# Attention sums of a graph network: one-hot tiles split between ScalarE and VectorE, all loads issued by SyncE into rings of eight

## The reference

```
a  = exp(a - amax[edge_dst])                                   # one weight per edge and head
ns = segment_sum(vs * a / segment_sum(a)[dst], edge_dst)       # 64 scalar features
nv = segment_sum(vv * a / segment_sum(a)[dst], edge_dst)       # 32 vectors of 3 components
```

## Time and profile before

| what | value |
|---|---|
| median of 3 runs | 12143.02 us (12134.39 to 12146.55) |
| profiled execution, its own time | 12142.17 us |
| profiled execution, its span | 12140.4 us |
| busy over the whole span: PE, DVE, ACT, POOL | 73%, 71%, 36%, 66% |
| mean granted TensorE clock | 0.808 |
| mean DMA rate | 109 GB/s |

### The profile page before, as it was taken

One profiled execution on the slowest core, in us unless ns is written; L12 is line 12 of the kernel. 1 busy time (PEld: TensorE's weight loads), 2 busy tenths in 40 slices (PEclk: granted clock), 3 DMA queues, 4 the chain that ended last, 5 costly groups with the idle time before them and its releaser, 6 DMA issues. The chain is left out here.

```text
span 12140.4 us, 219938 instructions
## 1 busy us (share of the span) xinstructions
PE 8894.9 (73%) x44805; PEld 7005.1 (58%) x44805; DVE 8560.0 (71%) x21214; ACT 4341.0 (36%) x10856; POOL 8069.6 (66%) x8212
## 2 busy tenths in 40 slices
PE   2899999992665666666666558888888465799995
PEld 2788888881555422222222447777777454566664
DVE  4677777778763455555555349999999876688874
ACT  1455555551002222222222126666666300344431
POOL 4788888883653488888888127777777364477760
PEclk7777787776985677777777569999999798799995
DMA  3455554443650288888888423333333374233331
GB/s 93 104 115 113 115 113 114 114 112 114 187 146 18 56 131 131 131 132 132 131 132 131 153 85 87 92 93 91 92 91 92 82 183 127 69 103 104 103 98 41
DMA packets 1350642, 1320.15 MB, mean 109 GB/s; under 512 B 508622, under 2 KB 1147330, under 8 KB 1349894
## 3 DMA queue, kind: packets, MB, share of 16 engines
q0 software_dynamic: 347904, 594.12, 26.5%
q1 hardware_dynamic: 854716, 713.61, 21.3%
q10 hardware_dynamic: 147914, 11.21, 0.9%
HBM read 800.64 MB, written 517.55 MB: 109 GB/s over the span
## 5 line engine op out<-in xcount | busy, mean ns | idle before, releaser
L737 POOL DMA_INDIRECT e_gd<-tab_dst,e_ix x1568 | 1732.2, 1105 | 477.8 <-issue 477.5
L737 POOL DMA_INDIRECT e_gs<-tab_src,e_ix x1568 | 1640.0, 1046 | 501.3 <-issue 436.3
L788 PE MATMUL e_psS<-e_rows,e_same 128*128 128x480 f32 x1568 | 1116.6, 878 | 863.1 <-DVE e_same L762 863.1
L676 PE MATMUL e_psF<-w_ident,e_F 128*128 128x128 f32 x6272 | 1264.6, 310 | 245.3 <-ACT e_F L1954 232.7
L806 POOL DMA_INDIRECT acc<-e_sums,e_row x784 | 1249.2, 1593 | 238.8 <-issue 205.0
L788 PEld LDWEIGHTS e_psS<-e_rows,e_same 128*128 128x128 f32 x1568 | 431.8, 293 | 1555.6 <-issue 1526.5
L706 ACT ACTIVATE e_FT<-e_psF 128x384 f32<-128x384 f32 (+1 forms) x2352 | 1072.0, 456 | 569.9 <-PE e_psF L676 552.9
L1563 PE MATMUL s_psS<-s_wv,s_hot 128*128 128x168 f32 (+1 forms) x3904 | 726.1, 335 | 585.0 <-POOL s_wv L1521 560.2
L1772 POOL DMA_INDIRECT e_g<-tab_src,e_er x976 | 962.7, 986 | 279.3 <-issue 225.8
L676 PEld LDWEIGHTS e_psF<-w_ident,e_F 128*128 128x128 f32 x6272 | 876.1, 166 | 377.6 <-issue 336.4
L1563 PEld LDWEIGHTS s_psS<-s_wv,s_hot 128*128 128x128 f32 x3904 | 619.5, 207 | 691.3 <-issue 478.9
(11 more groups left out here) (492 smaller groups left out, 24828.6 us busy)
## 6 DMA issues: line engine op xcount, KB each, us to landing
s_val<-val SPq DMA_DIRECT2D x488, 320.0 KB
val<-e_O SPq DMA_DIRECT2D x392, 320.0 KB
acc<-w_zeros SPq DMA_DIRECT2D x392, 139.5 KB
n_ag<-acc SPq DMA_DIRECT2D x56, 960.0 KB
e_krow<-in_src_t SPq DMA_DIRECT2D x196, 256.0 KB
sums<-e_total SPq DMA_DIRECT2D x244, 192.0 KB, 1.9
e_es<-in_es SPq DMA_DIRECT2D x196, 130.0 KB
e_gs<-tab_src,e_ix POOLq DMA_INDIRECT x1568
```

Source lines behind the costliest of these rows:

```text
L676: last = nc.tensor.transpose(psF[:, P * g:P * g + P], F[:, k, P * g:P * g + P], ident[:, :])
L737: pool.indirect_dma_start(into[t][u][:, k, :], None, tables[t], bass.IndirectOffsetOnAxis(ix[u][:, t, k:k + 1], 0))\
L788: nc.tensor.matmul(psS[(k) % len(psS)], T["same"][u][:, k, :], values[:, k, :], start=True, stop=True)\
```

## The change

Three things change inside `attention_sums`; nothing outside it does.

1. The one-hot tiles. ACT now makes three of the four: for each, one activation writes the absolute difference of lane and target, and one further activation over all three turns that into max(0, 1 - difference), which is 1 where they are equal and 0 elsewhere. DVE makes the first tile with a compare of 128x128. Lane and target are kept as floats for this; POOL shifts the targets in place and then copies them into the float tile.
2. The weight products. DVE makes all four parts; POOL keeps the copy of the weights.
3. The loads. SP issues `key`, `pb` and `val` of a step, ACT issues none. The tiles that are loaded, and the totals, stand in rings of RING = 8, the others in rings of HALF = 4. Weighting stands four steps behind the loads, the store ten. The hardware loop has eight steps to a turn, and 16 steps are unrolled ahead of it.

```diff
-        RING = 4
+        RING, HALF = 8, 4
         val, pb, key = ring("val", [P, TM, CX], RING), ring("pb", [P, TM, H], RING), ring("key", [P, TM], RING, I32)
-        rel, hot, wv = ring("rel", [P, TM], RING, I32), ring("hot", [P, TM, P], RING), ring("wv", [P, TM, width], RING)
+        rel, hot, wv = ring("rel", [P, TM], HALF), ring("hot", [P, TM, P], HALF), ring("wv", [P, TM, width], HALF)
...
-        SUM, TOTAL, STORE, LAST = 1, 3, 7, 7
+        REL, APART, HOT, WEIGH, SUM, TOTAL, STORE, LAST = 2, 3, 4, 4, 5, 7, 10, 10
...
         @block.sync
                 if m := i_of(0):
-                    wait_apart(sp, sem("weighted_s"), i - RING + 1, sem("sp_passed"))
-                    wait_apart(sp, sem("weighted_v"), i - RING + 1, sem("sp_passed"))
+                    wait_apart(sp, sem("weighted"), i - RING + 1, sem("sp_passed"))
                     at = sp.value_load(W["block"][0:1, bass.ds(i, 1)], min_val=0, max_val=NM - 1)
+                    wait_apart(sp, sem("rel"), i - RING + 1, sem("sp_passed"))
+                    wait_apart(sp, sem("copied"), i - RING + 1, sem("sp_passed"))
+                    sp.dma_start(key[u][:, :], block_at(targets, at)).then_inc(sem(f"key{u}"), 16)
+                    sp.dma_start(pb[u][:, :, :].rearrange("p t h -> p (t h)"), block_at(weights, at)).then_inc(sem(f"in{u}"), 16)
                     sp.dma_start(val[u][:, :, :].rearrange("p t c -> p (t c)"), block_at(values, at)).then_inc(sem(f"in{u}"), 16)
...
         @block.gpsimd
+                if m := i_of(REL):
+                    wait_apart(pool, sem(f"key{u}"), (j + 1) * 16, sem("pool_passed"))
+                    wait_apart(pool, sem("apart"), i - HALF + 1, sem("pool_passed"))
+                    wait_apart(pool, sem("hot_first"), i - HALF + 1, sem("pool_passed"))
+                    nc.gpsimd.tensor_tensor(key[u][:, :], key[u][:, :], W["shift"][:, bass.ds(i, 1)].to_broadcast([P, TM]), ALU.add)\
+                        .then_inc(sem("shifted"), 1)
+                    wait_apart(pool, sem("shifted"), i + 1, sem("pool_passed"))
+                    nc.gpsimd.tensor_copy(rel[u % HALF][:, :], key[u][:, :]).then_inc(sem("rel"), 1)
+                if m := i_of(WEIGH):
+                    wait_apart(pool, sem(f"in{u}"), (j + 1) * 32, sem("pool_passed"))
+                    wait_apart(pool, sem("summed"), i - HALF + 1, sem("pool_passed"))
+                    nc.gpsimd.tensor_copy(wv[u % HALF][:, :, CX:width], pb[u][:, :, :]).then_inc(sem("copied"), 1)
...
         @block.vector
+                if m := i_of(WEIGH):
+                    dve.wait_ge(sem(f"in{u}"), (j + 1) * 32)
+                    wait(dve, sem("summed"), i - HALF + 1)
+                    scalars = lambda t: t[:, :, 0:C0].rearrange("p t (h c) -> p t h c", h=H)
+                    tt(scalars(wv[u % HALF]), scalars(val[u]), bcast(pb[u][:, :, :], 3, C0 // H), ALU.mult)
+                    for d in range(3):
+                        part = lambda t: t[:, :, C0 + C1 * d:C0 + C1 * d + C1].rearrange("p t (h c) -> p t h c", h=H)
+                        last = tt(part(wv[u % HALF]), part(val[u]), bcast(pb[u][:, :, :], 3, C1 // H), ALU.mult)
+                    last.then_inc(sem("weighted"), 1)
                     dve.wait_ge(sem("rel"), i + 1)
-                    tt(hot[u][:, :, :], bcast(W["lane"][:, :], 1, TM), bcast(rel[u][:, :], 2, P), ALU.is_equal).then_inc(sem("hot"), 1)
+                    nc.vector.tensor_scalar(hot[u % HALF][:, 0, :], lane[:, :], rel[u % HALF][:, 0:1], None, ALU.is_equal).then_inc(sem("hot_first"), 1)
...
         @block.scalar
-                    at = act.value_load(W["block"][0:1, bass.ds(i, 1)], min_val=0, max_val=NM - 1)
-                    act.dma_start(key[u][:, :], block_at(targets, at)).then_inc(sem(f"in{u}"), 16)
-                    act.dma_start(pb[u][:, :, :].rearrange("p t h -> p (t h)"), block_at(weights, at)).then_inc(sem(f"in{u}"), 16)
+                if m := i_of(APART):
+                    act.wait_ge(sem("rel"), i + 1)
+                    wait(act, sem("summed"), i - HALF + 1)
+                    for k in range(1, TM):
+                        last = nc.scalar.activation(hot[u % HALF][:, k, :], lane[:, :], ACT.Abs, bias=rel[u % HALF][:, k:k + 1], scale=-1.0)
+                    last.then_inc(sem("apart"), 1)
+                if m := i_of(HOT):
+                    act.wait_ge(sem("apart"), i + 1)
+                    nc.scalar.activation(hot[u % HALF][:, 1:TM, :], hot[u % HALF][:, 1:TM, :], ACT.Relu, bias=1.0, scale=-1.0).then_inc(sem("hot"), 1)
```

More of the change, by code:

```diff
@@ L1472, in attention_sums @@
         ring = lambda name, shape, n, dt=F32: [S.sb(f"{name}{u}", shape, dt) for u in range(n)]
-        RING = 4
+        RING, HALF = 8, 4
         val, pb, key = ring("val", [P, TM, CX], RING), ring("pb", [P, TM, H], RING), ring("key", [P, TM], RING, I32)
-        rel, hot, wv = ring("rel", [P, TM], RING, I32), ring("hot", [P, TM, P], RING), ring("wv", [P, TM, width], RING)
-        total = ring("total", [P, width], RING)
-        psS = [S.ps(f"psS{u}", [P, 512]) for u in range(RING)]
+        rel, hot, wv = ring("rel", [P, TM], HALF), ring("hot", [P, TM, P], HALF), ring("wv", [P, TM, width], HALF)
+        total, lane = ring("total", [P, width], RING), S.sb("lane", [P, P])
+        psS = [S.ps(f"psS{u}", [P, 512]) for u in range(HALF)]
         values, weights = blocks_of(D["val"]), blocks_of(D["probs"][H])
         targets = D["dst_sorted"].rearrange("p t -> (p t)").rearrange("(m q k) -> m q k", q=P, k=TM)
-        SUM, TOTAL, STORE, LAST = 1, 3, 7, 7
+        REL, APART, HOT, WEIGH, SUM, TOTAL, STORE, LAST = 2, 3, 4, 4, 5, 7, 10, 10
         block = ctx.enter_context(nc.Block())
-        def weigh(tt, u, a, n):
-            heads = lambda t: t[u][:, :, a:a + n].rearrange("p t (h c) -> p t h c", h=H)
-            return tt(heads(wv), heads(val), bcast(pb[u][:, :, :], 3, n // H), ALU.mult)
         @block.sync
@@ L1505, in _ @@
             for u in range(RING):
-                sp.wait_ge(sem(f"stored{u}"), 16 * (V // RING))
+                sp.wait_ge(sem(f"stored{u}"), 16 * -(-(V - u) // RING))
         @block.gpsimd
         def _(pool):
-            tt = nc.gpsimd.tensor_tensor
             def body(i_of):
-                if m := i_of(0):
+                if m := i_of(REL):
                     i, u, j = m
[L1515 to L1521, removed]
+                    wait_apart(pool, sem(f"key{u}"), (j + 1) * 16, sem("pool_passed"))
[6 more added lines that the diff above has]
+                if m := i_of(WEIGH):
+                    i, u, j = m
+                    wait_apart(pool, sem(f"in{u}"), (j + 1) * 32, sem("pool_passed"))
+                    wait_apart(pool, sem("summed"), i - HALF + 1, sem("pool_passed"))
+                    nc.gpsimd.tensor_copy(wv[u % HALF][:, :, CX:width], pb[u][:, :, :]).then_inc(sem("copied"), 1)
             steps(pool, V, LAST, body, RING)
@@ L1545, in body @@
                     nc.vector.scalar_tensor_tensor(out=total[u][:, :], in0=total[(u - 1) % RING][:, :], scalar=W["keep"][:, bass.ds(i, 1)],
-                                                   in1=psS[u][:, 0:width], op0=ALU.mult, op1=ALU.add).then_inc(sem("totals"), 1)
+                                                   in1=psS[u % HALF][:, 0:width], op0=ALU.mult, op1=ALU.add).then_inc(sem("totals"), 1)
             dve.wait_ge(sem("empty"), 1)
+            dve.wait_ge(sem("lane"), 1)
             steps(dve, V, LAST, body, RING)
@@ L1557, in body @@
                     i, u, j = m
-                    wait_apart(pe, sem("weighted_v"), i + 1, passed)
+                    wait_apart(pe, sem("copied"), i + 1, passed)
                     wait_apart(pe, sem("hot"), i + 1, passed)
-                    wait_apart(pe, sem("weighted_s"), i + 1, passed)
-                    wait_apart(pe, sem("totals"), i - RING + 1, passed)
+                    wait_apart(pe, sem("hot_first"), i + 1, passed)
+                    wait_apart(pe, sem("weighted"), i + 1, passed)
+                    wait_apart(pe, sem("totals"), i - HALF + 1, passed)
                     for k in range(TM):
-                        last = nc.tensor.matmul(psS[u][:, 0:width], hot[u][:, k, :], wv[u][:, k, :], start=(k == 0), stop=(k == TM - 1))
+                        last = nc.tensor.matmul(psS[u % HALF][:, 0:width], hot[u % HALF][:, k, :], wv[u % HALF][:, k, :],
+                                                start=(k == 0), stop=(k == TM - 1))
                     last.then_inc(sem("summed"), 1)
@@ L1569, in _ @@
         def _(act):
+            nc.scalar.activation(lane[:, :], W["lane"][:, :], ACT.Copy).then_inc(sem("lane"), 1)
             def body(i_of):
-                if m := i_of(0):
+                if m := i_of(APART):
                     i, u, j = m
-                    wait_apart(act, sem("rel"), i - RING + 1, sem("act_passed"))
-                    wait_apart(act, sem("weighted_s"), i - RING + 1, sem("act_passed"))
```

(10 more changed lines are left out.)

## The result

The changed kernel takes 12623.09 us (median of 4 runs, 12607.34 to 12637.12) against 12144.78 us: a ratio of 1.0395, 95% interval 1.0382 to 1.0408. The forecast was 12670 in a range of 12550 to 12785, so the direction held and the forecast was 47 us too high. The profiled execution has a span of 12605.6 us, 465.2 more than before.

A forecast was written before the change was run, and what follows sets the result against it. SP's own instruction stream was taken to set the pace: 224 steps x 3.44 us plus unrolled steps and tail make 828.4 us, +264.0 per stage; twice that, 12142.2 + 528 = 12670 us (formula 11129 + 448 s), range 12550 to 12785.

The forecast's parts named there:

- SP's missing L79: SP's waits in the loop stand at source line L79; no profile row has it, so SP never waits for a buffer there.
- The moved loads: SP's loop step: issuing key and pb, moved from ACT, adds 0.53 us each, +1.06 us a step (1.02 to 1.38).
- The step: SP's loop step: 2.31 + 1.06 for loads + 0.10 for waits - 0.03 for the loop's end = 3.44 us.
- the register load: SP's read of the block's number in each step: stays at 0.40 us; its extremes shift the step by -0.14 or +0.20.
- The low end of the step: SP's loop step with all low ends together: 2.31 + 1.02 + 0.02 - 0.03 - 0.14 = 3.18 us, or 12554 us.
- the high end: SP's loop step with both loads bringing a wait along: 2.31 + 1.38 = 3.69 us, or 12782 us.
- The deeper rings and SP's new waits: Loop: eight buffers and earlier loads gain nothing; new waits never hold, as 16.1 us fits in eight steps, 27.5 us.
- The computing: Loop work per step hidden under SP's 3.44 us: DVE 1.92 us, ACT 1.61, PE 1.50, or 2.8 at the lower clock.
- The first: Rival, loop: transfers bind and eight buffers free them; DVE's 1.92 us sets the step, -181, 11961 us; chance 0.05.
- The second: Rival, loop: SP's register work overlaps the added issues, the step stays at 2.31 us, time 12142 us; chance 0.02.
- The third rival: ACT's loop: alternating functions each cost a table load of 1.283 us; step 4.18 us, time 13002 us; chance 0.03.
- The fourth: Rival, SP's loop: the copied or rel wait holds SP beyond a 27.5 us buffer turn; at 30 us, 12809 us; chance 0.03.

## Why the prediction was right

**What bounds the kernel.** SP's missing L79 was the right row to rest on. Three experiments confirm that the pace is the issuing: more issues lengthen the step load by load, less register work shortens it with as many transfers, and deeper rings alone do nothing.

**The moved loads.** +1.06 was forecast for the two; the trace of the changed kernel shows 0.52 each, 1.04.

**The step.** 3.44 was forecast, 3.29 measured. The term that was mis-sized is the register load, which I had let stay as it was: its median fell from 0.397 to 0.317 us, its longest from 0.599 to 0.408, and the mean over all of them in the two stretches from 0.421 (223 loads) to 0.315 (183 loads). That is 0.11 of the 0.15; 0.01 to 0.02 are the two loads, the rest is small change in the waits and at the loop's end. Why the register load became shorter is open. The low end of the step, 3.18, had -0.14 for it; the high end, 3.69, left out the +0.20 that is named beside it. 448 x 0.15 = 67 us would by the formula give 12603; the median is 20 above that, and the profiled execution, 12607, nearly on it.

**The deeper rings and SP's new waits.** Worth nothing and costing nothing, as forecast: no wait of SP in the loop.

**The computing.** Hidden, as forecast, but some prices were off. The one-hot compare on DVE took 0.280 us, not 0.226, and ACT's passes 0.391, not 0.367:

```profile
L1587 ACT ACTIVATE s_hot<-s_lane,s_rel 128x128 f32<-128x128 f32 x546 | 179.3, 391 | 344.3 <-POOL s_rel L1518 331.7 <-PE s_psS L1571 12.6
...
L1544 DVE TENSOR_SCALAR s_hot<-s_lane,s_rel 128x128 f32<-128x128 f32 x183 | 51.2, 280 | 0.0
```

Busy shares were forecast too high (DVE 56%, measured 46%; ACT 47%, measured 42%), since durations of instructions that overlap were added up: DVE's busy time is 1.53 us a step and not 1.92. PE's forecast of 44% assumed a steady clock; the clock fell, and 72% with a longer step is 434.75 / 600 x 3.29 = 2.38 us, inside the bound of 2.8.

**The rivals.** The first, transfers freed by eight buffers, falls with the run of rings alone. The second, a step that stays at 2.31 us, falls with the 3.29. The two rules of the Trainium skill that were set against the forecast do not hold for this stage. The Trainium skill, Perfetto Trace Analysis, section on what "DMA-bound" means, looks for a queue solid with DMA slices. Here SP's DMA slices fill 0.69 of 2.31 us before and about 1.36 of 3.29 after, and the queue is the bound in both. The Trainium skill, DMA: Bandwidth & Descriptors, section "Issuing engines are not separate DMA queues", calls the sequencer's time usually small beside the transfer. Here a load costs SP 0.52 us, for 2 KB and for 16 KB alike, and this is what lengthens the step. The third rival is out as well: no table load stands in ACT's loop, and its last pass keeps its 0.507. The fourth needed a wait on SP that no row shows.

## What to carry to other kernels

When engines wait for a transfer, look next at the queue that issues it: if that queue never waits itself, more buffers and earlier loads cannot help, and every instruction moved onto it is paid in full, its register reads and address work too. Count the whole instruction stream of an issuing queue, not its DMA instructions; here those filled 30% of the step before and 41% after. The second queue was better used here in turns of whole steps than for two loads of every step (1.09% under the kernel before with rings of four, 1.85% with rings of eight), since each queue then reads the block's number only every second step; and only then did the depth of the rings matter.

## What the runs showed of the hardware that was not expected

- The register load of one number takes different times on SP from kernel to kernel, by its median: 0.272 us in the turns with rings of four, 0.314 and 0.317 with the new division of the computing, 0.338 and 0.455 with two loads and one load moved, 0.383 in the turns with rings of eight, 0.397 in the kernel before, 0.522 with rings of eight alone. The means lie closer together, from 0.28 to 0.46. In these stretches it is always between 0.26 and 0.67. What stretches it was not settled; it does not follow the transfer rate, which was 220 GB/s in the shortest case and 186 in the longest.
- The mean granted TensorE clock of a stretch, which lies between the levels of 1.2 GHz (0.5) and 2.4 GHz (1.0), fell as the step grew longer in which PE does the same eight matmuls: 1.00 with a step of 1.82 us, 0.94 at 2.31, 0.76 at 2.87, 0.57 at 3.29 and 0.52 at 3.45.
- POOL's copy of the weights takes 0.204 us on average in the kernel before (3100 to 3400 us) and 0.474 in the turns with rings of eight, for the same 128x32 elements; POOL had no idle time in the latter. The turns with rings of four hold both kinds: of 70 copies with no weight product of DVE in their first 0.2 us none took over 0.21 us, of the 82 with such a product 62 took over 0.3. With the split and the loads on ACT only 7 of 70 such copies did, so what decides it is open.
